# Attention scores from two 12-bit float32 parts in 64-row halves, in place of three bfloat16 parts in 32-column strips

## The chip, the cores and the metric

The kernel runs on one core of a Trainium2 chip, in one launch. The metric is the device time of that core in microseconds (us). Three runs of the kernel before gave 1925.89 us in the median, 1922.76 us at the lowest and 1926.48 us at the highest. TensorE multiplies matrices (PE in the profile; PEld is its loading of the stationary operand), VectorE (DVE), ScalarE (ACT) and GpSimd (POOL) work on rows of 128 partitions, and SyncE (SP) issues DMAs.

## The reference

Four layers of attention and a feed-forward part over 2048 tokens of width 128 follow one another; each adds attention times a gate to its input. The change lies in the two layers with 16 heads of width 8, layer 0 (all keys) and layer 3 (causal, with rotary positions). All is float32.

```python
def _L0_attn_ref(x, Wq, bq, Wk, bk, Wv, bv, Wo, bo):        # 16 heads, d = 8, T = 2048
    q, k, v = proj(Wq, bq), proj(Wk, bk), proj(Wv, bv)
    scores = jnp.einsum('bhtd,bhsd->bhts', q, k) * scale
    attn = jax.nn.softmax(scores, axis=-1)
    out = jnp.einsum('bhts,bhsd->bhtd', attn, v)
def _L3_attn_ref(x, qw, kw, vw, ow):
    Q, K = rope(Q, freq), rope(K, freq)
    score = jnp.einsum('bhqd,bhkd->bhqk', Q, K) / scale
    score = score - 10000000000.0 * (1.0 - causal)
    score = score - jnp.max(score, axis=-1, keepdims=True)
    weights = jax.nn.softmax(score, axis=-1)
    attn = jnp.einsum('bhqk,bhkd->bhqd', weights, V)
```

## The kernel before

`head_projections` makes q and k for all heads (128 rows, 8 per head) in eight blocks of 512 columns and splits each float32 number into three bfloat16 parts: ScalarE rounds the number (L403) and the rest (L407), VectorE subtracts (L446, L452). Six DMAs (L336) write the parts to memory outside the chip's buffers. `attention_heads` then runs the 16 heads. For one head, `load_stacks` puts the parts one above the other on 72 partitions, so that one product over 72 rows is the exact sum of the nine products of parts; `qs` holds the queries, `ks` the keys. In layer 0 a second pair, `qd` and `kd`, has the first 64 rows again on partitions 64 to 127.

Each head is gone through twice. The first pass finds the maximum of every query's scores. `fill` multiplies 128 queries by a block of 512 keys into `pM`: in layer 0 over 64 rows, two blocks side by side in the two halves of TensorE's rows (L747), in layer 3 over 72 rows, as four matmuls of 32 columns each (`by_columns`, L725). VectorE's `take` reduces the result (L881 over two blocks in layer 0, L892 and L889 over one in layer 3). `pM` has four banks in layer 0 and three in layer 3, and `fill` waits for the `take` that frees its bank. The 16 x 128 maxima of a head are split in three (`split_max`), turned by TensorE (`turn`, L757), copied by ScalarE (`keep_rows`, L837) and put by three DMAs (L639) on rows 72 to 74 of `qs`, where `ks` has ones: the second pass has the maximum subtracted by the product itself.

The second pass, `score_chunk`, multiplies 128 keys by 512 queries over 75 rows into `pS` (L725, four matmuls of 32 columns), ScalarE's exponential (L856) writes `probs`, and `sum_unit` multiplies four of those chunks by the values in float32, each chunk in a 32-column strip of its own (L787). A float32 product is two MATMUL records per strip. Four chunks are a unit; a head has 16 units in layer 0 and 10 in layer 3. `pS` has three banks: a score waits for the exponential three before it. In the causal layer a product with `neg_below` is added to a chunk that crosses the diagonal.

The order of TensorE's instructions is written out in `one_head` of the tensor block: the sums of unit u, then four scores (one of unit u+1 and three of unit u+2), with fills of the next head put between them at the places in `behind`. In layer 0 a unit has two fills: both behind the second score in even units, behind the first and the third in odd ones. In layer 3 a unit has three to five, and where there are four or more the last stands behind the fourth score, right before the next sums.

## Time and profile before

| | us |
|---|---|
| median of three runs | 1925.89 |
| lowest to highest | 1922.76 to 1926.48 |
| span of the profiled execution | 1923.2 |
| TensorE, VectorE, ScalarE busy in it | 1697.7, 1435.9, 1143.8 |

The profiled execution's time is its span of 1923.2 us from the first to the last instruction; the page gives nothing outside it, and the median of the runs is 2.7 us more. The heads of layer 0 run from about 55 to 740 us, those of layer 3 from about 1401 to 1840 us. TensorE's busy time counts a matmul from its start to its modelled end, so matmuls that follow one another overlap: the distance between two starts tells what a matmul costs in a stream, its duration does not. In the rows, an engine's name with a q (SPq) is its queue of DMA issues, and the bracket at a row's end is the idle time before it and what ended that.

### The profile page before, as it was taken

What the parts mean: (1) busy time and instruction counts of PE and PEld (TensorE: products, weight loads), DVE (VectorE), ACT (ScalarE), POOL (GpSimd) and SP (SyncE); (2) the same over time, 40 slices, a digit from 0 to 9 for tenths busy, and PEclk for the clock granted to TensorE, in tenths of its full rate; (3) what the DMA queues carried; (4) which work ended last, traced back from release to release, by engine and by line L of the source; (5) the groups of instructions that cost most, each with busy time, mean ns of one, the idle gap of its engine ahead of it and who ended that gap; (6) DMA issues with size and microseconds to landing.
All of it is one profiled execution on the core that took longest, in us unless ns stands there. A gap on an engine that the chain in (4) does not pass through costs nothing. (4 is left out here: it accounts for less than half of the span.)

```text
span 1923.2 us, 44062 instructions
## 1 busy us (share of the span) xinstructions
PE 1697.7 (88%) x17529; PEld 802.7 (42%) x17529; DVE 1435.9 (75%) x2718; ACT 1143.8 (59%) x2262; POOL 307.7 (16%) x460
## 2 busy tenths in 40 slices
PE   3799999999999995889997798892779999999977
PEld 2222222222222222434444544781425555555556
DVE  5889999999999954665555507656779999999735
ACT  3268888888888894332222244452317777777754
POOL 0103000010000100000000345443012232210123
PEclk8789999999999998799997899996759999999988
DMA  4112111121111012033233269861511111111132
GB/s 143 36 30 81 63 55 51 55 81 64 55 51 34 28 28 59 33 66 106 95 89 144 69 225 333 268 186 48 191 33 30 33 37 37 34 36 36 28 76 70
DMA packets 78037, 154.52 MB, mean 80 GB/s; under 512 B 18684, under 2 KB 35964, under 8 KB 74136
## 3 DMA queue, kind: packets, MB, share of 16 engines
q1 hardware_dynamic: 63034, 121.38, 20.0%
q0 software_dynamic: 14384, 29.29, 4.9%
q8 instruction: 139, 2.28, 0.5%
q10 hardware_dynamic: 414, 1.04, 0.2%
q14 instruction: 66, 0.54, 0.1%
HBM read 102.23 MB, written 48.89 MB: 79 GB/s over the span
## 5 line engine op out<-in xcount | busy, mean ns | idle before, releaser
L856 ACT ACTIVATE heads_probs<-heads_pS 128x512 f32<-128x512 f32 (+3 forms) x1664 | 851.6, 573 | 187.9 <-PE heads_pS L725 172.2
L881 DVE TENSOR_REDUCE heads_run_max<-heads_pM 128x1 f32<-128x1024 f32 x512 | 592.6, 1216 | 54.6 <-PE heads_pM L747 53.3
L787 PE MATMUL heads_pO<-heads_probs,heads_vh 128*32 128x512 f32 (+2 forms) x3328 | 438.1, 570 | 3.2 <-ACT heads_probs L856 1.4
L725 PE MATMUL heads_pS<-heads_qs,heads_ks 75*32 75x512 bf16 (+3 forms) x4160 | 392.7, 370 | 3.8 <-ACT heads_probs L856 1.6
L892 DVE TENSOR_REDUCE heads_run_max<-heads_pM 128x1 f32<-128x512 f32 x384 | 246.7, 684 | 17.2 <-PE heads_pM L725 13.7
L725 PE MATMUL heads_pS<-heads_q_first,heads_ks 75*32 75x512 bf16 x2496 | 234.4, 377 | 7.9 <-ACT heads_probs L856 7.4
L725 PEld LDWEIGHTS heads_pS<-heads_qs,heads_ks 75*32 75x32 bf16 x4160 | 117.3, 95 | 171.2 <-issue 81.3
L725 PE MATMUL heads_pM<-heads_ks,heads_qs 72*32 72x512 bf16 (+3 forms) x1600 | 174.6, 359 | 1.1 <-DVE heads_run_max L892 0.5
L889 DVE CUSTOM_DVE_ANT_0 heads_masked_out<-heads_pM,heads_mask_end 128x128 bf16<-128x128 f32 (+3 forms) x256 | 120.7, 485 | 19.5 <-PE heads_pM L725 17.2
L787 PEld LDWEIGHTS heads_pO<-heads_probs,heads_vh 128*32 128x32 f32 x3328 | 106.7, 110 | 53.3 <-issue 7.1
L725 PEld LDWEIGHTS heads_pS<-heads_q_first,heads_ks 75*32 75x32 bf16 x2496 | 71.3, 95 | 122.4 <-ACT heads_probs L856 66.8
L1404 ACT ACTIVATE top_act_gate<-top_pG 128x512 f32<-128x512 f32 x68 | 40.6, 597 | 137.3 <-PE top_pU L1360 137.3
L617 POOL DMA_DIRECT2D k_head_out_dram<-heads_ot x120 | 62.9, 531 | 356.9 <-DVE heads_ot L912 230.4
L747 PE MATMUL heads_pM<-heads_ks,heads_qs 64*128 64x512 bf16 x320 | 114.3, 393 | 4.7 <-DVE heads_run_max L881 4.7
L747 PE MATMUL heads_pM<-heads_kd,heads_qd 64*128 64x512 bf16 x320 | 114.3, 393 | 0.0
L725 PE MATMUL heads_pM<-heads_ks,heads_q_first 72*32 72x512 bf16 (+3 forms) x960 | 106.7, 383 | 7.9 <-DMA heads_ks<-k_parts_dram 6.7
L1438 DVE TENSOR_TENSOR top_hidden<-top_act_gate,top_pU 128x512 f32<-128x512 f32 x68 | 46.7, 687 | 76.8 <-ACT top_act_gate L1404 76.8
L2115 POOL DMA_INDIRECT k_x_slots_dram<-k_xn,k_place_i x32 | 31.1, 973 | 381.6 <-DVE k_place_i L1984 358.3
L725 PE MATMUL heads_pS<-k_neg_below,k_ident_b 128*32 128x128 bf16 x1024 | 90.7, 222 | 0.0
L1616 DVE TENSOR_REDUCE second_row_max<-second_banks 128x1 f32<-128x2048 f32 (+15 forms) x16 | 20.7, 1291 | 90.4 <-PE second_banks L1574 90.4
L725 PEld LDWEIGHTS heads_pM<-heads_ks,heads_qs 72*32 72x32 bf16 x1600 | 62.5, 97 | 59.3 <-DVE heads_run_max L892 19.1
L747 PEld LDWEIGHTS heads_pM<-heads_ks,heads_qs 64*128 64x128 bf16 x320 | 29.6, 93 | 133.4 <-DVE heads_run_max L881 86.7
(388 smaller groups left out, 2369.0 us busy)
## 6 DMA issues: line engine op xcount, KB each, us to landing
top_weights<-k_comb_dram SPq DMA_DIRECT2D x128, 128.0 KB, 3.0
second_w<-in_L_W_dram SPq DMA_DIRECT2D x12, 1024.0 KB, 10.8
k_hid_slots_dram<-k_zeros SPq DMA_DIRECT2D x8, 1152.0 KB, 5.0
k_h_slots_dram<-second_work SPq DMA_DIRECT2D x48, 192.0 KB, 3.1
second_work<-k_hid_slots_dram SPq DMA_DIRECT2D x48, 192.0 KB, 4.3
k_parts_dram<-proj_part SPq DMA_DIRECT2D x12, 512.0 KB, 4.1
heads_ks<-k_parts_dram SPq DMA_DIRECT2D x63, 96.0 KB
heads_qs<-k_parts_dram SPq DMA_DIRECT2D x40, 96.0 KB
```

The costliest lines, as they stand in the source:

```text
L617: queue.dma_start(K.head_out[h, :, b * BLK:(b + 1) * BLK], ot[c][b * 32:b * 32 + HD + 1, 0, :])\
L725: mm = pe.matmul(out[cols, :], still[:, cols], moving, start=start, stop=stop)
L747: mm = pe.matmul(pM[:, bank_of(c, j, k), 0:w], (qs, qd)[k][c % ROUND][rows, i * P:(i + 1) * P], (ks, kd)[k][c % ROUND][rows, b * BLK:b * B ...
L787: mm = pe.matmul(pO[k * 32:k * 32 + VW, int(second), o:BLK], vh[c][:, t, :], probs[u % 2][:, k * BLK + o:(k + 1) * BLK], start=first_chunk ...
L856: act.activation(probs[u % 2][:, k * BLK + c0 - b * BLK:(k + 1) * BLK], pS[:, slot, 0:c1 - c0], ACT.Exp)\
L881: dve.reduce_max(run_max[:, i, blocks[0][0] // 2:blocks[0][0] // 2 + 1], both.rearrange("p k c -> p (k c)"), AX.X).then_inc(taken, 2)
L889: dve.tensor_tensor_reduce(masked_out[:, i % TPB, 0:w], pM[:, bank, 0:w], mask_end[:, BLK - w:BLK], 1.0, LOWEST, ALU.add, ALU.max, run_max ...
L892: dve.reduce_max(run_max[:, i, b:b + 1], pM[:, bank, 0:w], AX.X).then_inc(taken, 1)
L1404: act.activation(act_gate[:, m % 2, :], pG[:, m % 2, :], ACT.Silu).then_inc(gated, 1)
L1438: mix = dve.tensor_tensor(hidden[:, m % 2, :], act_gate[:, m % 2, :], pU[:, m % 2, :], ALU.mult)
L1616: chain(dve.reduce_max(self.row_max[:, i:i + 1], self.scores_row[:, 0:(i + 1) * P], AX.X))
L2115: pool.indirect_dma_start(out=K.x_slots[k], out_offset=bass.IndirectOffsetOnAxis(ap=K.place_i[:, c, t:t + 1], axis=0), in_=K.xn[:, t, :], ...
```

## The change

Each number is split in two parts of 12 significant bits, held as float32 and declared as `float32r` (`ROUNDED`). VectorE masks the low bits (`HIGH_BITS`) and subtracts; ScalarE copies the masked part. Four products of parts make 32 rows (`STK`). Every head's stack lies twice, on partitions 0 to 63 and 64 to 127, and `fill` and `score_chunk` use the two halves in turn (`turns`). Row 32 is zero in the queries and one in the keys; the three rows of maxima are 33 to 35, written in both halves by six DMAs. `fill` multiplies over 33 rows, `score_chunk` over 36, each as one matmul of 128 columns; `by_columns`, `qd` and `kd` go. The causal mask is two bfloat16 products over one half's 64 rows, the second with the other half's mask (`ident_swapped`, `neg_below_swapped`). A head's stacks are 6 DMAs where there were 14 in layer 0 and 8 in layer 3. The spare rows are set by four memsets per buffer, on VectorE for the first buffer and GpSimd for two others, in place of one each. In layer 0 both fills of a unit stand behind its second score in every unit.

```diff
+ROUNDED = mybir.dt.float32r
...
 PARTS = 3
-STK = PARTS * PARTS * HD
+SPLIT = 2
+HIGH_BITS = -4096
+STK = SPLIT * SPLIT * HD
+HALF = 64
+MAX_ROW = STK + 1
...
-        parts = [[S.sb(f"part{w}{a}", [P, T], BF16) for a in range(PARTS)] for w in range(2)]
+        parts = [[S.sb(f"part{w}{a}", [P, T], ROUNDED) for a in range(SPLIT)] for w in range(2)]
...
+                for a, done in enumerate((hi, lo)):
                     sp.wait_ge(done, NB * (w + 1))
-                    sp.dma_start(K.parts[w][:, a, :, :], parts[w][a][:, :]).then_inc(stored[w], 16)
+                    sp.dma_start(K.parts[w][:, a, :, :], parts[w][a][:, :].bitcast(F32)).then_inc(stored[w], 16)
...
-                if n < N:
-                    act.wait_ge(whole, n + 1)
-                    act.activation(parts[w][0][:, cols], full[:, n % 4, :], ACT.Copy).then_inc(hi, 1)
                 if n >= 1:
                     w, b = divmod(n - 1, NB)
-                    act.wait_ge(r1, n)
-                    act.activation(parts[w][1][:, b * BLK:(b + 1) * BLK], rest[:, (n - 1) % 4, :], ACT.Copy)\
-                       .then_inc(mid, 1)
+                    act.wait_ge(masked, n)
+                    act.activation(parts[w][0][:, b * BLK:(b + 1) * BLK], rest[:, (n - 1) % 4, :], ACT.Copy)\
+                       .then_inc(hi, 1)
...
-                    w, b = divmod(n, NB)
-                    dve.wait_ge(hi, n + 1)
+                    dve.wait_ge(whole, n + 1)
                     if n >= 4:
-                        dve.wait_ge(lo, n - 3)
-                    dve.tensor_tensor(rest[:, n % 4, :], full[:, n % 4, :], parts[w][0][:, b * BLK:(b + 1) * BLK],
-                                      ALU.subtract).then_inc(r1, 1)
+                        dve.wait_ge(hi, n - 3)
+                    dve.tensor_scalar(rest[:, n % 4, :].bitcast(I32), full[:, n % 4, :].bitcast(I32), HIGH_BITS, None,
+                                      ALU.bitwise_and).then_inc(masked, 1)
                 if n >= 1:
                     w, b = divmod(n - 1, NB)
-                    cols = slice(b * BLK, (b + 1) * BLK)
-                    dve.wait_ge(mid, n)
-                    dve.tensor_tensor(parts[w][2][:, cols], rest[:, (n - 1) % 4, :], parts[w][1][:, cols],
-                                      ALU.subtract).then_inc(lo, 1)
+                    dve.wait_ge(masked, n)
+                    dve.tensor_tensor(parts[w][1][:, b * BLK:(b + 1) * BLK], full[:, (n - 1) % 4, :],
+                                      rest[:, (n - 1) % 4, :], ALU.subtract).then_inc(lo, 1)
...
 def first_queries(K, causal):
 
-    at = 0
-    for _, n0, n1 in PRODUCTS:
-        rows = at + (n1 - n0) * HD
-        for first in (0,) if causal or at >= HALF else (0, HALF):
-            yield K.first_q[first // HALF][first + at:first + rows, :], K.parts[0][0, n0:n1].rearrange("a d t -> d a t")
-        at = rows
+    for half in (0, HALF):
+        yield K.first_q[half:half + STK, :].bitcast(F32), query_parts(K, 0)
...
-        qs = [K.first_q[0]] + [S.sb(f"qs{i}", [P, T], BF16) for i in range(1, ROUND)]
-        ks = [S.sb(f"ks{i}", [P, T], BF16) for i in range(ROUND)]
-
-        qd = None if causal else [K.first_q[1]] + [S.sb(f"qd{i}", [P, T], BF16) for i in range(1, ROUND)]
-        kd = None if causal else [S.sb(f"kd{i}", [P, T], BF16) for i in range(ROUND)]
+        qs = [K.first_q] + [S.sb(f"qs{i}", [P, T], ROUNDED) for i in range(1, ROUND)]
+        ks = [S.sb(f"ks{i}", [P, T], ROUNDED) for i in range(ROUND)]
...
-        LOADS = 8 if causal else 14
+        LOADS, SPARE_ROWS = 6, 4
...
-            h, at = ROUND * p + c, 0
-            for r, n0, n1 in PRODUCTS:
-                n = n1 - n0
-                q = K.parts[0][h, n0:n1].rearrange("a d t -> d a t")
-                k = K.parts[1][h, r].unsqueeze(1).broadcast_to([HD, n, T])
-                for first in (0,) if causal or at >= HALF else (0, HALF):
-                    rows = slice(first + at, first + at + n * HD)
-                    for full, half, src in ((qs, qd, q), (ks, kd, k)):
-                        yield (half if first else full)[c % ROUND][rows, :], src, stacked[c % ROUND]
-                at += n * HD
+            h = ROUND * p + c
+            for half in (0, HALF):
+                yield qs[c % ROUND][half:half + STK, :].bitcast(F32), query_parts(K, h), stacked[c % ROUND]
+                for r in range(SPLIT):
+                    rows = slice(half + r * SPLIT * HD, half + (r + 1) * SPLIT * HD)
+                    yield ks[c % ROUND][rows, :].bitcast(F32), key_part(K, h, r), stacked[c % ROUND]
...
+        def set_spare_rows(engine, i):
+
+            for n, (stack, half) in enumerate(itertools.product((qs[i], ks[i]), (0, HALF))):
+                rows = slice(half + HALF // 2, half + HALF)
+                engine.memset(stack[rows, :].bitcast(F32), float(n // 2)).then_inc(rows_set[i], 1)
+                engine.wait_ge(rows_set[i], n + 1)
...
-                for a in range(PARTS):
-                    sp.dma_start(qs[c % ROUND][STK + a:STK + a + 1, :].rearrange("o (t c) -> o t c", c=P),
-                                 max_rows[a * NT:(a + 1) * NT, :]).then_inc(rows_in, 16)
+                for row in (MAX_ROW, HALF + MAX_ROW):
+                    for a in range(PARTS):
+                        sp.dma_start(qs[c % ROUND][row + a:row + a + 1, :].bitcast(F32).rearrange("o (t c) -> o t c", c=P),
+                                     max_rows[a * NT:(a + 1) * NT, :].bitcast(F32)).then_inc(rows_in, 16)
...
                     for i, (dst, src, sem) in enumerate(load_stacks(p, c + 2)):
-                        sp.wait_ge(scored, EVENTS * (ROUND * p + c) + 2 + 2 * i)
+                        sp.wait_ge(scored, EVENTS * (ROUND * p + c) + 2 + 4 * i)
                         sp.dma_start(dst, src).then_inc(sem, 16)
...
         @block.tensor
         def _(pe):
-            def by_columns(out, still, moving, start, stop):
-
-                for g in range(P // VW):
-                    cols = slice(g * VW, (g + 1) * VW)
-                    mm = pe.matmul(out[cols, :], still[:, cols], moving, start=start, stop=stop)
-                return mm
+            turns = itertools.cycle((0, HALF))
...
@@ -733,19 +728,15 @@
                 n = BLOCKS * (ROUND * p + c) + before[j + 1]
                 i, blocks, _ = runs[j]
                 if j == 0:
+                    pe.wait_ge(rows_set[c % ROUND], SPARE_ROWS)
                     pe.wait_ge(stacked[c % ROUND], 16 * LOADS * (p + c // ROUND + 1))
                 if not isinstance(n, int) or n > FILLED:
                     pe.wait_ge(taken, n - FILLED)
-                if causal:
-                    (b, w), = blocks
-                    bank = pM[:, bank_of(c, j, 0), :]
-                    mm = by_columns(bank[:, 0:w], qs[c % ROUND][0:STK, i * P:(i + 1) * P],
-                                    ks[c % ROUND][0:STK, b * BLK:b * BLK + w], True, True)
-                else:
-                    for k, (b, w) in enumerate(blocks):
-                        rows = slice(k * HALF, (k + 1) * HALF)
-                        mm = pe.matmul(pM[:, bank_of(c, j, k), 0:w], (qs, qd)[k][c % ROUND][rows, i * P:(i + 1) * P],
-                                       (ks, kd)[k][c % ROUND][rows, b * BLK:b * BLK + w], start=True, stop=True)
+                for k, (b, w) in enumerate(blocks):
+                    at = next(turns)
+                    rows = slice(at, at + STK + 1)
+                    mm = pe.matmul(pM[:, bank_of(c, j, k), 0:w], qs[c % ROUND][rows, i * P:(i + 1) * P],
+                                   ks[c % ROUND][rows, b * BLK:b * BLK + w], start=True, stop=True)
                 mm.then_inc(filled, 1)
...
                 diag = causal and c0 == u * P
-                mm = by_columns(pS[:, slot, 0:c1 - c0], ks[c % ROUND][0:STK + PARTS, u * P:(u + 1) * P],
-                                qs[c % ROUND][0:STK + PARTS, c0:c1], True, not diag)
+                at = next(turns)
+                rows, mask = slice(at, at + MAX_ROW + PARTS), slice(at, at + HALF)
+                mm = pe.matmul(pS[:, slot, 0:c1 - c0], ks[c % ROUND][rows, u * P:(u + 1) * P],
+                               qs[c % ROUND][rows, c0:c1], start=True, stop=not diag)
                 if diag:
-                    mm = by_columns(pS[:, slot, 0:P], K.ident_b[:, :], K.neg_below[:, :], False, True)
+                    pe.matmul(pS[:, slot, 0:P], K.ident_b[mask, :], K.neg_below[mask, :], start=False, stop=False)
+                    mm = pe.matmul(pS[:, slot, 0:P], K.ident_swapped[mask, :], K.neg_below_swapped[mask, :], start=False,
+                                   stop=True)
                 mm.then_inc(scored, 1)
...
                     else:
 
-                        behind = [(len(new) // 2, 1 + 2 * i)[u % 2] for i in range(len(todo))]
+                        behind = [len(new) // 2] * len(todo)
...
-            dve.memset(ks[0][64:96, :], 1.0).then_inc(ones_set[0], 1)
+            set_spare_rows(dve, 0)
```

The first place is TensorE's queue in layer 0, from one unit's sums to the next (an odd unit before). heads_pO are the sums, heads_pS the scores, heads_pM the maxima's products. Before:

```order
L787 MATMUL heads_pO<-heads_probs,heads_vh 32x512 x4
L725 MATMUL heads_pS<-heads_q_first,heads_ks 32x512 x4
L747 MATMUL heads_pM<-heads_ks,heads_qs 128x512
L747 MATMUL heads_pM<-heads_kd,heads_qd 128x512
L725 MATMUL heads_pS<-heads_q_first,heads_ks 32x512 x8
L747 MATMUL heads_pM<-heads_ks,heads_qs 128x512
L747 MATMUL heads_pM<-heads_kd,heads_qd 128x512
L725 MATMUL heads_pS<-heads_q_first,heads_ks 32x512 x4
L787 MATMUL heads_pO<-heads_probs,heads_vh 32x512 x4
```

The same stretch of the changed kernel:

```order
L782 MATMUL heads_pO<-heads_probs,heads_vh 32x512 x4
L764 MATMUL heads_pS<-heads_q_first,heads_ks 128x512 x2
L738 MATMUL heads_pM<-heads_ks,heads_qs 128x512 x4
L764 MATMUL heads_pS<-heads_q_first,heads_ks 128x512 x2
L782 MATMUL heads_pO<-heads_probs,heads_vh 32x512 x4
```

The four strips of a score are one matmul now, and the four products for the maxima stand together between the second and the third score; sums in 32-column strips stand between work of 128 columns on both sides.

The second place is TensorE's queue in layer 3, up to the sums of a unit with a fill right before them. Before:

```order
L725 MATMUL heads_pM<-heads_ks,heads_q_first 32x512 x4
L725 MATMUL heads_pS<-heads_qs,heads_ks 32x256 x4
L725 MATMUL heads_pS<-k_neg_below,k_ident_b 32x128 x4
L725 MATMUL heads_pM<-heads_ks,heads_q_first 32x512 x4
L725 MATMUL heads_pS<-heads_qs,heads_ks 32x512 x4
L725 MATMUL heads_pM<-heads_ks,heads_q_first 32x512 x4
L787 MATMUL heads_pO<-heads_probs,heads_vh 32x384 x2
```

The same place of the changed kernel:

```order
L738 MATMUL heads_pM<-heads_ks,heads_qs 128x512
L764 MATMUL heads_pS<-heads_qs,heads_ks 128x256
L767 MATMUL heads_pS<-k_neg_below,k_ident_b 128x128
L768 MATMUL heads_pS<-k_neg_below_swapped,k_ident_swapped 128x128
L738 MATMUL heads_pM<-heads_ks,heads_qs 128x512
L764 MATMUL heads_pS<-heads_qs,heads_ks 128x512
L738 MATMUL heads_pM<-heads_ks,heads_qs 128x512
L782 MATMUL heads_pO<-heads_probs,heads_vh 32x384 x2
```

The order of fills and scores is the same; all of them were in 32-column strips like the sums, and none is now.

## Rows read from the trace of the kernel before

**Rows 1.** Engine totals of 50 us in the heads of layer 0 and of layer 3:
```profile
200.00:250.00 50.00, 50.00 (x565) 14.41 (x561) 46.36 (x42) 43.90 (x83) 3.21 (x9) 1.00 0.16 52
...
1650.00:1700.00 50.00, 49.62 (x902) 28.23 (x898) 45.97 (x123) 36.73 (x80) 6.28 (x12) 1.00 0.12 27
```

**Rows 2.** Timeline of layer 0, two units; start us, us, engine line:
```profile
400.19 1.03 PE L787 MATMUL heads_pO<-heads_probs,heads_vh 128*32 128x512 f32 x8
...
401.59 0.39 PE L747 MATMUL heads_pM<-heads_ks,heads_qs 64*128 64x512 bf16 x1
...
401.82 0.38 PE L747 MATMUL heads_pM<-heads_ks,heads_qs 64*128 64x512 bf16 x1
...
404.62 0.09 PEld L747 LDWEIGHTS heads_pM<-heads_ks,heads_qs 64*128 64x128 bf16 x1 [0.42 <-DVE heads_run_max L881]
...
404.94 0.40 PE L725 MATMUL heads_pS<-heads_qs,heads_ks 75*32 75x512 bf16 x4
...
405.17 0.60 PE L787 MATMUL heads_pO<-heads_probs,heads_vh 128*32 128x512 f32 x4
```

**Rows 3.** Timeline of VectorE, maxima of layer 0 with every bank full:
```profile
71.06 22.71 DVE L881 TENSOR_REDUCE heads_run_max<-heads_pM 128x1 f32<-128x1024 f32 x20 [0.17 <-PE heads_pM L747]
```

**Rows 4.** Timeline of the last head of layer 0, TensorE:
```profile
705.78 0.40 PE L725 MATMUL heads_pS<-heads_qs,heads_ks 75*32 75x512 bf16 x4 [0.27 <-ACT heads_probs L856]
...
706.01 1.03 PE L787 MATMUL heads_pO<-heads_probs,heads_vh 128*32 128x512 f32 x8
...
706.87 0.39 PE L725 MATMUL heads_pS<-heads_qs,heads_ks 75*32 75x512 bf16 x4
...
707.96 0.40 PE L725 MATMUL heads_pS<-heads_q_first,heads_ks 75*32 75x512 bf16 x4 [0.27 <-ACT heads_probs L856]
```

**Rows 5.** Timeline of ScalarE, layer 3, once per head:
```profile
1585.30 0.27 ACT L837 ACTIVATE heads_max_rows<-heads_pS 48x128 bf16<-48x128 bf16 x1 [0.71 <-PE heads_pS L757]
...
1611.33 0.27 ACT L837 ACTIVATE heads_max_rows<-heads_pS 48x128 bf16<-48x128 bf16 x1 [0.71 <-PE heads_pS L757]
```

**Rows 6.** Timeline of TensorE, bf16 maxima and then f32 products:
```profile
63.05 0.38 PE L747 MATMUL heads_pM<-heads_ks,heads_q_first 64*128 64x512 bf16 x1
...
63.36 0.49 PE L963 MATMUL heads_pS<-k_squares,heads_probs 128*128 128x128 f32 x2
...
63.68 0.39 PE L964 MATMUL heads_pS<-k_rows_of,k_ident 128*128 128x128 f32 x2
...
63.91 0.39 PE L963 MATMUL heads_pS<-k_squares,heads_probs 128*128 128x128 f32 x2
```

**Rows 7.** Timeline of layer 1, f32 products behind a wait and in stream:
```profile
920.26 1.12 PE L1368 MATMUL top_pY<-top_hidden,k_down 128*128 128x512 f32 x2 [0.54 <-DVE top_hidden L1444]
...
921.22 1.02 PE L1359 MATMUL top_pG<-k_xnT,k_gate 128*128 128x512 f32 x2
...
922.08 1.02 PE L1360 MATMUL top_pU<-k_xnT,k_up 128*128 128x512 f32 x2
```

**Rows 8.** Timeline, layer 0, from the maxima's transpose to the next head:
```profile
300.98 1.84 SPq L639 DMA_DIRECT2D heads_qs<-heads_max_rows  x3
...
305.71 0.61 PE L725 MATMUL heads_pS<-heads_qs,heads_ks 75*32 75x512 bf16 x8
```

**Rows 9.** What the loads of the maxima (L639) took in layer 0:
```profile
DMA to landing us min/median/max: 1.7/1.7/3.3
```

**Rows 10.** Timeline, layer 3, start of the heads stage:
```profile
1400.29 0.11 DVE L923 MEMSET heads_run_max<- 128x64 f32 x1
...
1401.71 1.85 PE L725 MATMUL heads_pM<-heads_ks,heads_q_first 72*32 72x128 bf16 x24 [6.71 <-DMA heads_ks<-k_parts_dram]
```

**Rows 11.** Groups of instructions of the first 50 us:
```profile
L403 ACT ACTIVATE proj_part<-proj_full 128x512 bf16<-128x512 f32 x8 | 5.0, 630 | 0.3
...
L114 DVE MEMSET k_zeros<- 128x2304 f32 x1 | 2.0, 1978 | 1.3 <-PEq L2606 1.3
L917 DVE MEMSET heads_ks<- 32x2048 bf16 x1 | 1.8, 1765 | 3.5 <-PEq L65 3.5
```

57 lines of the change are left out of this document (28 added, 29 removed).

## The prediction

> **What bounds the kernel now.** I read the engine totals in stretches first, then the timeline of each of the two heads stages, then the nearest relatives of what the change adds. In the heads of layer 0 TensorE is busy in all 50.00 us of 50, VectorE in 46.36, ScalarE in 43.90; in layer 3 it is 49.62, 45.97 and 36.73 [rows 1]. TensorE's share alone says little, since its matmuls overlap, so the timeline decides. In layer 0 the sums of one unit start at 400.19 us and those of the second unit after it at 405.17: 2.49 us a unit [rows 2]. VectorE could go faster: with every bank full it does 20 reductions of 1024 in 22.71 us, 1.14 us each, 2.27 us a unit [rows 3]. What would be left without the maxima is seen in the last head, where nothing is filled: the score in front of the sums starts at 705.78, the next such score at 707.96, a cycle of 2.18 us [rows 4]. It is closed: that score waits for an exponential, the sums follow 0.23 us behind it, the next score 0.86 us behind the sums' start, and 1.09 us later the exponential of that score has released the next one. So a unit in layer 0 costs 2.49 us through TensorE's own stream, with 2.27 (VectorE) and 2.18 (the cycle) right below it. In layer 3 a head takes 1611.33 - 1585.30 = 26.03 us, 2.60 us for each of ten units [rows 5]. There a maximum's product of 512 columns stands between the last score and the sums in most units, so the cycle is 2.18 + 0.21 = 2.39 us (the granted clock is 1.00, the level of 2.4 GHz [rows 1], and 512 columns at that are 0.21 us); the other 0.21 are masks, narrow pieces and the turn of a head.
>
> **Part 1: the width of the products.** In a stream, two pairs of bf16 products of 64 rows and 512 columns start 0.23 us apart [rows 2], and the two of a pair run together. The new products are of a type that the trace doesn't show. The nearest rows below are these bf16 pairs (one pass over the columns), above them the f32 products, whose two records cost 922.08 - 921.22 = 0.86 us, four passes [rows 7]. A part has only 12 bits, and nothing in the change calls for a second half of it, so I take one pass, and I take it that two products in different halves overlap as the bf16 pairs do. Then eight products of a unit in layer 0 take four times 0.21 us where six slots did the same before (four scores, two pairs): TensorE's stream falls by 0.43 us a unit and is no bound any more. What comes next is the cycle through the sums.
>
> **Part 2: what the cycle gets longer by.** Before, scores and sums were both in 32-column strips in both layers; now sums stand between products of 64 rows and 128 columns. (a) From products of one shape to the other costs 0.10 us: a bf16 pair is started at 404.62, the strips behind it at 404.94, 0.32 us in place of the 0.23 between two pairs [rows 2]. (b) The way back is dearer, since the stationary operand is four bytes wide: bf16 products at 63.05, f32 at 63.36 (0.31, so 0.10 again), and the next at 63.68, 0.32 us behind in place of the 0.23 from there to 63.91 [rows 6]. 0.10 + 0.10 = 0.20 us. (c) The score in front of the sums waits for its exponential, and only then can its weights be loaded. For f32 that shows: 920.26 to 921.22 is 0.96 us behind a wait, 0.86 in the stream [rows 7], 0.10 us; for bf16 it doesn't (the load at 404.62 ends a wait for VectorE [rows 2], and the 0.32 from there to the next product is 0.01 more than the 0.31 of a pair that hadn't waited [rows 6]). I take 0.10. Together 0.10 + 0.20 + 0.10 = 0.40 us, and the cycle is 2.18 + 0.40 = 2.58 us. The bounds of (b) and (c): if the new type's weights load as bf16 does, the load costs 0 in both and the sum is 0.20; if in (a) the sums' weights also have to be loaded with nothing beside them, 0.10 more, 0.50.
>
> The Trainium skill (TensorEngine Tiling (Array Packing), Key Properties) says that a change of tiling mode, other than one of tile, drains TensorE. The trace agrees, with the 0.10 us of [rows 2, 6]; by that rule alone, the cycle would be 2.38 us.
>
> The Trainium skill (TensorE: Matmul & The Clock Gate, Weight-path perf modes) says that the fast load of weights is on for 128 weights of a type other than FP32. The trace agrees as far as it goes: 0.10 us for f32, none for bf16 [rows 6, 7]; no run here shows on which side `float32r` stands. On the fast side the sum would be the one of rival B.
>
> **Part 3: the sum.** Layer 0: 2.58 - 2.49 = 0.09 us a unit, 15 heads of 16 units, +22 us. The last head has no maxima and goes from 2.18 to 2.58: 16 x 0.40 = +6. The maxima before the first head's scores are VectorE's [rows 3] and stay. Layer 3: the maximum's product between score and sums now runs beside the score, in the other half, but its weights are loaded behind the score's, 0.10 us (c). So the cycle goes from 2.39 to 2.68, +0.29 us; ten units and 15 heads, +44, and the last head +4. I keep the 0.21 of masks and narrow pieces as it is: the mask's two products are 0.05 us each in one half instead of one such, hidden where the other half has work. The order of layer 0's maxima costs and brings nothing, as TensorE has slack there.
>
> **Part 4: the ends.** Six DMAs of maxima in place of three: three are issued in 1.84 us [rows 8], six in 3.7, and one lands 1.7 us after its issue [rows 9], so the last lands at 300.98 + 3.05 + 1.7 = 305.7; the next head's first score is the second of those from 305.71 on [rows 8]. Just in time, 0; if they come late by all three issues, 1.84 x 30 heads = +55 is the far bound, nothing the near one. Memsets: VectorE sets 2304 columns of f32 in 1.98 us and 2048 of bf16 in 1.77 [rows 11], the same rate, so three more are 5.3 us. In layer 3 VectorE was ready at 1400.40, the first product started at 1401.71 [rows 10]: 1400.40 + 5.3 - 1401.71 = +4. In layer 0 the feed-forward products stand in front, 0. GpSimd's memsets are needed only when the second head's maxima start, some 20 us later. The projections lose one cast of 0.63 us for each of eight blocks [rows 11] and store 4 MB in place of 3: -5 to +3 for both layers, I take -3. The head stacks are 1 MB as before, at a DMA share of 0.16 and 0.12 [rows 1]: 0.
>
> Sum: 22 + 6 + 44 + 4 + 4 - 3 = +77 us on a span of 1923.2, 2000 us; the median of the runs is 2.7 us above that span, so 2003, rounded to 2000.
>
> **Rivals.** B, the loads don't show, on the other side: the new type's weights load like bf16. Cycle 2.38 us. Layer 0 gains 0.11 x 240 = 26 and loses 3 in the last head; layer 3 goes from 2.39 to 2.38, gains 2, loses 2; with the ends -22: 1904. If the change of shape costs nothing either, VectorE is the bound: 2.27 in layer 0 (-0.22 x 240 = -53) and 45.97 / 50 of the time in layer 3 (26.03 x 15 x 0.08 = -31), about 1842. B decides as soon as the cycle grows by less than 2.49 - 2.18 = 0.31 in layer 0 and 0.21 in layer 3. For it: only f32 rows show the load. Against: the operand is four bytes wide as theirs is. C, the halves don't overlap for this type (that the change doesn't do what it is laid out for): a unit of layer 0 is eight products of 0.21, sums of 0.86 and two changes, 1.7 + 0.86 + 0.3 = 2.86 us, +0.37 x 240 = 89; in layer 3 the maximum's product is in line again as before, and the rest grows by the 0.30 of the changes, +0.30 x 150 = 45; with the last heads' 10, 144, 2070. For it: nothing in the trace shows two four-byte products in halves. Against: eight records of f32 products in strips take 1.03 us together [rows 4]. D, two passes or more: a score of two passes is 0.21 us longer, and the cycle has two of them, before the sums and behind: 2.58 + 0.42 = 3.00 in layer 0 (+0.51 x 240 = 122) and 2.68 + 0.42 = 3.10 in layer 3 (+0.71 x 150 = 107), the last heads 26 x 0.82 = 21, so 2180; with four passes 250 more. E, gains and losses meet within 4 us, between A and B.
>
> **Chances.** My forecast A 0.46 (its own range 1970 to 2035), B 0.27, C 0.13, D 0.08, E 0.06. The time is A's, 2000. The range for 8 in 10 goes from 1895, which has B but for its far end, to 2070, where C is. A measurement of this kernel tells 0.2% (4 us) from no change. Faster 0.28, same 0.06, slower 0.66.
>
> **What would show it.** Right: in layer 0 the sums' starts are 2.5 to 2.65 us apart in every unit alike; the last head's cycle is near 2.58; ScalarE waits for TensorE's scores in each unit; VectorE is busy below 46 of 50 us; a head of layer 3 takes 28 to 29 us. B: the last head's cycle is 2.4 or less and VectorE is above 48 of 50. C: two scores side by side start 0.2 us apart, not 0.01. D: the same score's matmuls in one half start 0.4 us or more apart, or have two records. The forecast is wrong if the last head's cycle is not longer by 0.3 to 0.5 us.

## The result: 2645 us, 37% slower, at half of TensorE's clock

The changed kernel takes 2645.22 us (median of 4 runs, 2643.52 to 2646.26), the kernel before, on the same chip, 1926.18 us (4 runs, 1922.76 to 1927.63). The ratio is 1.374, with a 95% interval of 1.372 to 1.376. The forecast was 2000 us with a range to 2070: the sign was right, the size missed by 645 us.

The page's slices of the changed kernel show where to look. Each digit is a slice of 66 us, busy tenths of TensorE above, its granted clock in tenths below:

```profile
PE   3799999999999999977999698943999999999987
...
PEclk8555555555555555557999799976555555555558
```

Through the heads of layer 0 (slices 2 to 18) and of layer 3 (29 to 39) the clock is 0.50, the level of 1.2 GHz. TensorE is not idle there: in slices 3 to 17 and 29 to 38 it is busy in nine tenths and more. In windows (columns as in [rows 1]: PE, PEld, DVE, ACT, POOL, clock, DMA share, GB/s):

```profile
500.00:550.00 50.00, 50.00 (x199) 20.01 (x201) 29.48 (x27) 27.77 (x52) 3.20 (x9) 0.50 0.13 48
...
1300.00:1450.00 150.00, 148.40 (x354) 65.54 (x353) 84.53 (x132) 35.06 (x60) 0.00 (x0) 1.00 0.28 85
...
2000.00:2050.00 50.00, 50.00 (x230) 20.35 (x226) 28.21 (x74) 23.90 (x49) 7.37 (x11) 0.50 0.10 29
```

The middle one is layer 1, whose code the change leaves alone: clock 1.00. The outer two answer to [rows 1], where it was 1.00 too. VectorE and ScalarE, 46 and 44 of 50 before, are at 29 and 28: they wait for TensorE, ScalarE for 766 us in all (the last entry of this group of the page):

```profile
L851 ACT ACTIVATE heads_probs<-heads_pS 128x512 f32<-128x512 f32 (+3 forms) x1664 | 875.0, 571 | 799.4 <-PE heads_pS L764 766.0
```

The timeline of TensorE answers to [rows 2]; the first sums start at 500.21, the next at 504.28, so a unit (four chunks of scores and their sums) takes 4.07 us in place of 2.49. The last three rows are from layer 3:

```profile
500.21 1.93 PE L782 MATMUL heads_pO<-heads_probs,heads_vh 128*32 128x512 f32 x8
502.08 0.79 PE L764 MATMUL heads_pS<-heads_qs,heads_ks 36*128 36x512 f32 x2
502.67 1.05 PE L738 MATMUL heads_pM<-heads_ks,heads_qs 33*128 33x512 f32 x4
503.53 0.82 PE L764 MATMUL heads_pS<-heads_qs,heads_ks 36*128 36x512 f32 x2
504.28 1.08 PE L782 MATMUL heads_pO<-heads_probs,heads_vh 128*32 128x512 f32 x4
...
2051.05 0.62 PE L764 MATMUL heads_pS<-heads_qs,heads_ks 36*128 36x512 f32 x1
2051.05 0.62 PE L738 MATMUL heads_pM<-heads_ks,heads_qs 33*128 33x512 f32 x1
2051.48 0.62 PE L764 MATMUL heads_pS<-heads_qs,heads_ks 36*128 36x512 f32 x1
```

Even the sums, which are the same instructions as before, take 1.93 us in place of 1.03. The last three rows answer part 1 of the prediction: two products in different halves start together, and the next score in its half starts 0.43 us later. 512 columns at 1.2 GHz are 0.43 us: one pass. So rivals C and D are out, and what all the heads have in common is the clock; experiments 1 and 13 measure how much of the excess it is. A head of layer 3 takes 1955.57 - 1912.24 = 43.33 us (26.03 in [rows 5]):

```profile
1912.24 0.27 ACT L832 ACTIVATE heads_max_rows<-heads_pS 48x128 fp32r<-48x128 bf16 x1 [1.51 <-PE heads_pS L748]
1955.57 0.27 ACT L832 ACTIVATE heads_max_rows<-heads_pS 48x128 fp32r<-48x128 bf16 x1 [1.51 <-PE heads_pS L748]
```

One more wait is new. TensorE's waits, in total, times, longest:

```profile
PE heads_pM L738 <- DMA heads_ks<-k_parts_dram: 44.8, 2, 29.6
```

At the start of each of the two stages the first maximum waits for the stacks of keys, 15.1 us in layer 0 and 29.6 us in layer 3. In the kernel before that wait is 6.71 us in layer 3 [rows 10].

### The profile page after: what moved, and what is told of

Read it like the earlier page. It is cut to its first block and busy times, and to the rows that moved or that the text cites. A ratio compares the mean times of both kernels' runs of the same rounds, so it can differ in the third digit from the quotient of the medians.

```text
span 2642.9 us, 29151 instructions
## 1 busy us (share of the span) xinstructions
PE 2393.8 (91%) x10105; PEld 1100.5 (42%) x10105; DVE 1461.2 (55%) x2728; ACT 1159.3 (44%) x2246; POOL 328.2 (12%) x472
## 5 line engine op out<-in xcount | busy, mean ns | idle before, releaser
L782 PE MATMUL heads_pO<-heads_probs,heads_vh 128*32 128x512 f32 (+2 forms) x3328 | 804.6, 1012 | 1.4 <-ACT heads_probs L851 1.4
L764 PE MATMUL heads_pS<-heads_qs,heads_ks 36*128 36x512 f32 (+3 forms) x1040 | 497.6, 716 | 1.3 <-ACT heads_probs L851 1.3
L764 PEld LDWEIGHTS heads_pS<-heads_qs,heads_ks 36*128 36x128 f32 x1040 | 258.3, 302 | 451.4 <-ACT heads_probs L851 254.8
L738 PE MATMUL heads_pM<-heads_ks,heads_qs 33*128 33x512 f32 (+3 forms) x1040 | 390.0, 642 | 3.8 <-DVE heads_run_max L876 3.3
L764 PE MATMUL heads_pS<-heads_q_first,heads_ks 36*128 36x512 f32 x624 | 303.6, 717 | 6.6 <-ACT heads_probs L851 6.4
L738 PE MATMUL heads_pM<-heads_ks,heads_q_first 33*128 33x512 f32 x624 | 235.4, 647 | 53.3 <-DMA heads_ks<-k_parts_dram 44.8
L764 PEld LDWEIGHTS heads_pS<-heads_q_first,heads_ks 36*128 36x128 f32 x624 | 151.6, 301 | 287.8 <-ACT heads_probs L851 148.2
L738 PEld LDWEIGHTS heads_pM<-heads_ks,heads_qs 33*128 33x128 f32 x1040 | 214.7, 318 | 41.6 <-DVE heads_run_max L887 8.8
L738 PEld LDWEIGHTS heads_pM<-heads_ks,heads_q_first 33*128 33x128 f32 x624 | 126.9, 311 | 90.9 <-issue 49.2
L767 PE MATMUL heads_pS<-k_neg_below,k_ident_b 64*128 64x128 bf16 x256 | 83.7, 327 | 0.0
```

Of the source, the lines that this page charges most:

```text
L738: mm = pe.matmul(pM[:, bank_of(c, j, k), 0:w], qs[c % ROUND][rows, i * P:(i + 1) * P], ks[c % ROUND][rows, b * BLK:b * BLK + w], start=Tru ...
L764: mm = pe.matmul(pS[:, slot, 0:c1 - c0], ks[c % ROUND][rows, u * P:(u + 1) * P], qs[c % ROUND][rows, c0:c1], start=True, stop=not diag)
L767: pe.matmul(pS[:, slot, 0:P], K.ident_b[mask, :], K.neg_below[mask, :], start=False, stop=False)
L782: mm = pe.matmul(pO[k * 32:k * 32 + VW, int(second), o:BLK], vh[c][:, t, :], probs[u % 2][:, k * BLK + o:(k + 1) * BLK], start=first_chunk ...
```

## The experiments

They ran on four other chips than the first comparison: experiments 1 to 4 on one, 5 to 8, 9 to 12 and 13 to 15 on one each. The kernel before takes 1997.1, 1997.8, 1993.9 and 1999.5 us there, so every comparison below is with a run on one of these chips, and one across two of them can be off by up to 6 us. Experiments 9, 10, 11 and 15 have four to six runs each, the others one. "Unit" is the time from one unit's sums to the next in layer 0.

**1. All 64 rows of a half.** There are three theories of why the clock stays low. R: because a product has few rows (33 or 36) at work. T: because of the four-byte type. S: because the low level keeps itself, once the engine has waited.

```diff
-                    rows = slice(at, at + STK + 1)
+                    rows = slice(at, at + HALF)
...
-                rows, mask = slice(at, at + MAX_ROW + PARTS), slice(at, at + HALF)
+                rows, mask = slice(at, at + HALF), slice(at, at + HALF)
```

> Every product of a maximum and every score reads all 64 rows of its half (33 and 36 before); the spare rows hold zeros against ones, and in a maximum's product the rows of the head three back, which only shifts all scores of a row. Same records, same widths. Theory R (few rows of the array are at work, and so the granted clock stays at 0.50 in the heads): with 64 rows the clock is 1.00 again in 500-550 us of layer 0, a unit takes 2.4 to 2.7 us in place of 4.07, the kernel 1850 to 2070 us. Theory T (the four-byte type holds it down) and theory S (the slow level keeps itself, since the engine waits between its products): clock 0.50, unit 4.07 us, time 2640 within 15 us.

Measured: 2176.6 us, clock 1.00 in layer 0, unit 504.56 - 501.97 = 2.59 us. The spare rows hold zeros against ones, so they add nothing to a score (in a maximum's product, rows 33 to 35 hold the maxima of the head three back, which shift all scores of a query alike); that they are read is enough. The window of 50 us, and then the timeline of TensorE in this kernel:

```profile
500.00:550.00 50.00, 49.78 (x310) 18.27 (x306) 44.73 (x40) 40.43 (x80) 3.19 (x9) 1.00 0.18 70
```

```profile
501.97 1.06 PE L782 MATMUL heads_pO<-heads_probs,heads_vh 128*32 128x512 f32 x8
502.96 0.50 PE L764 MATMUL heads_pS<-heads_qs,heads_ks 64*128 64x512 f32 x2
503.30 0.82 PE L738 MATMUL heads_pM<-heads_ks,heads_qs 64*128 64x512 f32 x4
503.96 0.67 PE L764 MATMUL heads_pS<-heads_qs,heads_ks 64*128 64x512 f32 x2
504.56 1.07 PE L782 MATMUL heads_pO<-heads_probs,heads_vh 128*32 128x512 f32 x8
...
1691.22 0.44 PE L738 MATMUL heads_pM<-heads_ks,heads_qs 64*128 64x128 f32 x1 [5.11 <-issue]
```

So theory R holds, and the 2.59 is the 2.58 of my part 2. The total is above my 1850 to 2070, for layer 3 is still slow: its clock is 0.86 to 0.93, and once a head TensorE waits up to 5.4 us (62.9 us in 14 heads) in front of a maximum of the next stack but one, as in the last row. That is taken up in experiment 5.

**2. The type alone, and 3. type and rows.** Both operands are read as bf16 with a stride of two (`stack.bitcast(BF16)`, every second element), with 33 and 36 rows, and with 64. These two kernels leave the lower bits of every part out of the computation; only their times are of use.

> The same products with the same 33 and 36 rows in the same halves and the same order, but both operands are read as the upper two bytes of each element, bf16 with a stride of two (the lower bits are left out of the computation). Theory T (the type): clock 1.00, unit near 2.4 to 2.7 us, kernel 1850 to 2070 us. Theories R (rows) and S (keeps itself): clock 0.50; a unit of about 4 us, 2550 to 2650 us, and what it is shorter than 4.07 is what the loads of the wider type cost at the lower level.

> Both edits at once: bf16 operands read with a stride of two, and all 64 rows of the half. In the kernel before, pairs of such products stood among strips at a clock of 1.00 [rows 1, 2]. Theories R and T each say clock 1.00 here and 1850 to 2070 us; only theory S (the level keeps itself once the engine waits, whatever its operands are) says clock 0.50 and about 2600 us.

Measured: 2344.2 us with the few rows, 2114.2 us with 64. With the few rows the clock is 0.50 up to 530 us, and then, without any edit there, 1.00 up to the last head. Windows of that kernel:

```profile
300.00:350.00 50.00, 50.00 (x219) 9.63 (x213) 32.24 (x29) 29.70 (x56) 3.20 (x9) 0.50 0.06 23
...
600.00:650.00 50.00, 46.72 (x328) 10.02 (x326) 48.01 (x44) 43.41 (x85) 4.02 (x13) 1.00 0.13 48
```

My expectation for few rows (2550 to 2650) missed for this reason: with bf16 either level can hold for hundreds of us. So T is not refuted as a contribution, though the type alone doesn't bring the clock back for good. The total with 64 rows is above my 1850 to 2070, with the same waits in layer 3 as in experiment 1 (82.4 us in 14 heads). With 64 rows the clock is 1.00 throughout the heads of layer 0, and the unit is 2.41 to 2.42 us, the 2.38 of rival B. The loads of weights can explain the 0.17 between the two types (groups by shape, mean ns behind the busy time; first the kernel with 64 rows of the four-byte type, then bf16, then f32 products of layer 1 in the kernel before):

```profile
L764 PEld LDWEIGHTS heads_pS<-heads_q_first,heads_ks 64*128 64x128 f32 x64 | 9.1, 184 | 16.6 <-ACT heads_probs L851 16.3
```

```profile
L767 PEld LDWEIGHTS heads_pS<-heads_q_first,heads_ks 64*128 64x128 bf16 x31 | 2.3, 94 | 7.7 <-ACT heads_probs L854 7.5
```

```profile
L1368 PEld LDWEIGHTS top_pY<-top_hidden,k_down 128*128 128x128 f32 x72 | 13.4, 188 | 19.1 <-DVE top_hidden L1444 13.2 <-issue 3.3
```

That is 0.09 us for each load, and by part 2 two of them stand in a cycle with nothing beside them. Experiment 11 tests it: with stacks that really are bf16 the unit is 2.39 us.

**4. No halves, 128 rows.** Both copies are summed at once, which gives twice the score, and the exponential halves it: `rows = slice(0, P)`, `scale=0.5`. A maximum's product has 97 rows.

> No halves: each product reads rows 0 to 127 of the stacks (0 to 96 for a maximum), so both copies are summed at once, twice the score, and the exponential halves it. Products of 128 rows can't run beside each other. Theory R: 99 and 128 rows at work, clock 1.00; a unit of layer 0 is eight products of 0.21, sums 0.86, changes 0.3, so about 2.9 us, the kernel 2050 to 2150 us. Theories T and S: clock 0.50, a unit of 8 x 0.43 + 1.9 = 5.3 us or more, the kernel about 3000 us. If a product takes 0.86 us at a clock of 0.50, a product of 128 rows of this type needs two passes.

Measured: 2295.0 us, clock 1.00 in both layers, unit 503.89 - 500.83 = 3.06 us. Again theory R. The total is above my 2050 to 2150: I had left out the waits for the stacks (45.5 us at the two starts) and the slower chip, and the unit is 3.06 in place of my 2.9. It also shows what the halves are worth: 3.06 against 2.59 us.

**5. The loads of the stacks.** In the changed kernel a DMA of a stack has an outermost dimension of 2 (the copies). In a window of the changed kernel where nothing else is loaded (DMA share and GB/s are the last two numbers) the share of the 16 DMA engines is 0.13, which is 2 of 16:

```profile
60.00:66.00 6.00, 0.00 (x0) 0.00 (x0) 0.00 (x0) 0.00 (x0) 3.44 (x8) 0.50 0.13 52
```

The edit gives it the 8 rows of a part, as in the kernel before. A head then has eight loads of 16 rows in place of six, and its rows stand in another order:

```diff
-    return K.parts[0][h].rearrange("a d t -> (a d) t").unsqueeze(0).broadcast_to([SPLIT, SPLIT * HD, T])
+    return K.parts[0][h].rearrange("a d t -> d a t")
...
-    return K.parts[1][h, r].unsqueeze(0).broadcast_to([SPLIT, HD, T])
+    return K.parts[1][h, r].unsqueeze(1).broadcast_to([HD, SPLIT, T])
```

> The kernel with 64 rows in every product, and its stacks loaded in eight DMAs a head of 16 rows whose outermost dimension is the 8 rows of a part (six DMAs whose outermost dimension is 2 before; the rows of a stack stand in another order, the sums are the same). Theory L (a DMA is spread over as many engines as its outermost dimension allows, 2 of 16 before, so a head's 1 MB takes near 20 us and comes late): the wait of 16 us before the first maximum of each of the two layers falls below 5 us, the waits of 4 to 5 us in each head of layer 3 (62.9 us in 14) go, the kernel is 80 to 100 us shorter than 2176.6, so 2075 to 2095. Theory Q (the issues on SyncE, 1.57 us each for the keys, are what is late): the waits stay within a quarter of what they are, 2150 to 2190 us.

Measured: 2066.5 us, 110 less. TensorE no longer waits for stacks, layer 3's clock is 1.00, and a head of it takes 27.85 us where nothing disturbs it (1899.07 - 1871.12 = 27.95 below). Windows of this kernel (the first: the loads, at half of the DMA engines), then TensorE in the last head of layer 0, then ScalarE once per head of layer 3:

```profile
50.00:60.00 10.00, 8.43 (x19) 3.05 (x17) 7.80 (x8) 4.18 (x7) 9.71 (x6) 0.82 0.51 118
...
1800.00:1850.00 50.00, 47.06 (x352) 20.33 (x352) 42.69 (x114) 33.49 (x75) 5.96 (x11) 1.00 0.18 46
```

```profile
741.94 1.07 PE L782 MATMUL heads_pO<-heads_probs,heads_vh 128*32 128x512 f32 x8
...
744.55 0.64 PE L782 MATMUL heads_pO<-heads_probs,heads_vh 128*32 128x512 f32 x4
```

```profile
1871.12 0.27 ACT L832 ACTIVATE heads_max_rows<-heads_pS 48x128 fp32r<-48x128 bf16 x1 [0.64 <-PE heads_pS L748]
1899.07 0.27 ACT L832 ACTIVATE heads_max_rows<-heads_pS 48x128 fp32r<-48x128 bf16 x1 [0.64 <-PE heads_pS L748]
```

The total is below my 2075 to 2095. The edit changed the issues on SyncE too: the two of keys behind one another took 3.15 us in the kernel of experiment 1 (the row below), one takes 0.65 now. So it doesn't part L from Q by itself, but the row does: that load had been issued by 1678.48 + 3.15 = 1681.63 us, and the maximum that waited for it started at 1691.22, 9.6 us later. The transfer was late, not the issue.

```profile
1678.48 3.15 SPq L649 DMA_DIRECT2D heads_ks<-k_parts_dram  x2
```

At the start of layer 3 TensorE still sits idle for 19.6 us before its first maximum, now until VectorE's memsets are done (part 4 below). The Trainium skill (DMA: Bandwidth & Descriptors, Why a DMA increments its semaphore by 16 and not by 1) says that a DMA uses the largest number of engines up to 16 that divides the slowest dimension of both of its access patterns. The shares of 0.13 with 2 and 0.51 with 8 agree, and I had not applied it.

**6. A push at the start.** 40 products of 128 rows of f32 ahead of each layer's first head.

> The changed kernel, and in each of the two layers 40 products of 128 rows and 128 columns of f32 once, ahead of the first head's scores (their output is overwritten). Theory S (the level keeps itself, it only has to be brought up once): the clock is 1.00 behind them and stays so through the layer's heads, near 2.6 us a unit, 2100 to 2200 us. Theory R (rows): the clock goes to 1.00 during the 40 products at most and is back at 0.50 a few units later; the kernel takes 2640 to 2670 us.

Measured: 2723.5 us, above my 2640 to 2670; the changed kernel itself takes 2707.0 on another of these chips (14). Windows around the push:

```profile
132.00:136.00 4.00, 4.00 (x38) 3.88 (x37) 0.00 (x0) 0.00 (x0) 0.00 (x0) 1.00 0.00 0
136.00:140.00 4.00, 3.55 (x17) 1.11 (x17) 0.00 (x0) 3.54 (x7) 0.00 (x0) 0.99 0.06 16
140.00:144.00 4.00, 4.00 (x18) 1.58 (x18) 2.36 (x2) 2.17 (x4) 0.00 (x0) 0.50 0.14 57
```

The push ends at 135.9 us. TensorE waits once more, 0.45 us before the score at 137.03, and from there on not at all; up to 140 the clock is 0.99, behind it 0.50, with TensorE busy in all of the window. So raising the level once isn't enough: for the four-byte products of few rows theory S is out as a full account, since they let the clock fall from above.

**7. and 8. Only one of the two kinds with 64 rows.** One of the two lines of the first edit each.

> Only the products of the maxima read 64 rows, the scores stay at 36. Theory R with the sum of all rows deciding: four of eight products of a unit of layer 0 are full, the clock is at one level or the other for long stretches, mean between 0.6 and 0.9, 2250 to 2500 us. If either kind alone is enough, 2180 us; if both are needed, 2640.

> Only the scores read 64 rows, the products of the maxima stay at 33. In layer 0 this is the same number of wide products as with the maxima at 64 rows, so by the sum of all rows the same clock and time as there; in the last head of each layer, where only scores stand, the clock is 1.00.

Measured: 2232.0 and 2226.4 us. In layer 0 either alone is enough: clock 1.00 in 500:550 and a unit near 2.60 us in both. In layer 3 (1800:1850) it is 0.77 in both, below the 0.93 of experiment 1; but both kernels also wait for their stacks there (49.0 and 41.9 us), so these runs don't show what one kind alone would do in layer 3 without those waits. The last head of layer 0, where only scores stand, tells the two apart; the maxima with 64 rows, then the scores with 64 rows:

```profile
750.00:800.00 50.00, 46.23 (x160) 12.08 (x161) 1.75 (x1) 27.79 (x54) 2.08 (x4) 0.55 0.20 47
```

```profile
750.00:800.00 50.00, 42.65 (x242) 13.19 (x240) 9.04 (x8) 40.30 (x79) 2.91 (x8) 1.00 0.20 48
```

As soon as only 36-row scores are left, the clock falls; with 64-row scores it doesn't.

**9. Both mendings, and 10. both with the old order of the maxima.** The first is the kernel of experiment 5 once more. The second sets `behind` back to `[(len(new) // 2, 1 + 2 * i)[u % 2] for i in range(len(todo))]`.

> The kernel with 64 rows in every product and loads of eight outer rows once more, timed. By the single look (2064.6 us of span, the kernel before 1997.8 on the same chip) the ratio is 1.03; by the prediction's own sum (+77 us on 1923) it would be 1.04. If both mendings are all that the forecast had missed, the ratio lies between 1.025 and 1.045.

> The same kernel with layer 0's maxima in the order of the kernel before (every second unit takes its two runs of maxima behind the first and the third score). Theory N (the order is worth nothing, as I forecast, since the cycle through the sums decides): within 0.2% of the kernel with the new order. Theory O (the maxima's weight loads hide between scores that wait for their exponentials): a pair between two scores that wait anyway costs nothing, while the pair of sums' neighbours moves: up to 0.1 us in every second unit, 12 us faster. Theory P (a pair ahead of the score that the sums wait for makes the cycle longer in every second unit): 0.2 us in 120 units, 24 us slower.

Measured: 2069.5 and 2074.4 us, 1.0374 (1.0357 to 1.0391) and 1.0397 (1.0379 to 1.0414) of the kernel before. The 15 heads of layer 0, from the first keeping of maxima to the last, take 640.3 us in the new order and 639.7 in the old: in the place that it changes, the order is worth nothing. The 5 us between the totals, just over my 0.2%, lie elsewhere: of the 8.4 us between the two profiled spans, 4.7 are between the attention layers and 3.3 in layer 3, where both kernels have the same instructions. They were not looked into.

**11. Six products of bf16 parts.** A version that might beat both: parts and loads as in the kernel before, but six of the nine products of parts (the three smallest are left out of the sum), 48 rows, alternating halves, all 64 rows read.

```diff
+STACK = ((0, 0, 3), (1, 3, 2), (2, 5, 1))
+STK = 6 * HD
...
+                for r, at, n in STACK:
+                    rows = slice(half + at * HD, half + (at + n) * HD)
+                    yield qs[c % ROUND][rows, :], query_parts(K, h, n), stacked[c % ROUND]
+                    yield ks[c % ROUND][rows, :], key_part(K, h, r, n), stacked[c % ROUND]
```

> A version that might beat both: three bf16 parts as in the kernel before, but only six of the nine products of parts (48 rows, with the spare and the maxima's rows 64), in both halves of the array in turn and with all 64 rows at work; twelve loads a head with 8 outer rows. If the 0.17 us a unit between the four-byte stacks (2.59) and the bf16 reading of them (2.42) is the load of the wider weights, a unit of layer 0 takes 2.41 us against 2.49 in the kernel before, -19 us in 240 units, the last head +4; in layer 3 a head goes from 27.85 to about 26.0, which is what the kernel before takes. Ratio to the kernel before 0.985 to 1.0. If what costs 0.17 us is something else about the four-byte stacks' traffic, the unit stays at 2.59 and the ratio is 1.03.

Measured: 1988.9 us, ratio 0.9972 (0.996 to 0.9985), 0.3% less than the kernel before, with a unit of 2.39 us. So stacks that are bf16 give about what the bf16 reading of four-byte stacks gave (2.41), as it should be if the load of the wider weights is what costs the 0.2 us. In 14 heads the first score waits for its maxima's rows, 13.1 us in all, the place that my part 4 called just in time.

**12. The kernel before, here.**

> The kernel before itself, with a profile on the chip of these runs, where it takes 1997 us and not 1926 as in the first comparison. Theory G (the 70 us belong to the chip and lie in the stages between the two attention layers, where the runs with 64 rows also took about 50 us more than the changed kernel did in the first comparison): the units of layer 0 are 2.49 us apart as before and a head of layer 3 takes 26.0 us. Theory H (the heads are slower on this chip too): a unit is longer by more than 0.05 us, and then the units of the other kernels have to be read against it.

Measured: 1994.7 us. The 15 heads of layer 0 take 607.0 us (607.1 in the first comparison), those of layer 3 413.1 (396.2), and from the last keeping of maxima in layer 0 to the first in layer 3 it is 773.6 us (722.0). So 52 of the 70 us lie between the two attention layers, and theory G holds for layer 0 and not wholly for layer 3, where the first eight heads take 28 to 31 us each on this chip and the last seven 26.0 to 26.4. What these chips do more slowly there was not looked into.

**13. The loads mended, 33 and 36 rows kept, and 14. the changed kernel itself, here.**

> The changed kernel with its 33 and 36 rows, and only the loads of the stacks mended (eight a head, 8 outer rows). Theory R + L (rows set the clock, loads come late only where the heads are fast or just starting): clock 0.50 in the heads as before, the waits before the first maximum of each layer go (44.8 us in 2 to under 15), none in between, so 25 to 40 us shorter than the changed kernel on this chip, which I put at 2715. Theory I (the clock fell because the engine waited for loads): clock 1.00 in the heads and about 2070 us.

> The changed kernel itself on the chip of these runs. The kernel before is 68 us longer here than in the first comparison, in the stages between the two attention layers. If that is the chip and not the kernel, the changed kernel takes 2700 to 2725 us here, with the units of layer 0 4.07 us apart and the clock 0.50 in the heads as there. If the clock of the heads is a matter of the chip, it is not 0.50 here.

Measured: 2681.0 and 2707.0 us on one chip, clock 0.50 in the heads of both. The loads are worth 26 us at the lower level (at the two starts the first maximum waits 46.8 us for loads, and with the loads mended 20.1 for VectorE's memsets), and 110 at the upper one (experiments 1 and 5), where a head is short enough to run into them. A mending in the loads alone doesn't bring the clock back.

**15. The six products again, with fewer issues.** One DMA for three rows of maxima, and blocks placed so that no load waits for a memset: `qs[...][row:row + PARTS, :].rearrange("a (t c) -> a t c", c=P)` from `max_rows[:, :]`, `STACK = ((0, 0, 3), (2, 3, 1), (1, 6, 2))`.

> The six products of parts once more, with two edits: the rows of the smallest block stand at 24 and those of the middle one at 48, so that the spare rows 32 to 47 can be set without a wait of the loads for it; and the three rows of maxima go in one DMA for each half, 2 in place of 6 a head. If the issues on SyncE are what is late, the wait for the maxima's rows (13.1 us in 14 heads of layer 0) and about half of the 13.8 us at the start of layer 3 go: 15 to 25 us less than 1988.9, ratio to the kernel before 0.985 to 0.992. If one DMA of three rows is slower than three of one, by more than the 2.5 us saved in issues, the ratio stays at 0.997.

Measured: 1968.8 us (5 runs), ratio 0.9839 (0.9825 to 0.9854), 1.6% less than the kernel before. The wait for the maxima's rows is gone. Which of the two edits gave how much of the 20 us isn't separated. The window of layer 0, TensorE's timeline of one unit there, and that of the last head, which has no maxima:

```profile
500.00:550.00 50.00, 47.20 (x337) 9.88 (x329) 49.00 (x44) 43.66 (x86) 3.19 (x9) 1.00 0.15 50
```

```profile
501.86 1.07 PE L788 MATMUL heads_pO<-heads_probs,heads_vh 128*32 128x512 f32 x8
...
504.25 1.07 PE L788 MATMUL heads_pO<-heads_probs,heads_vh 128*32 128x512 f32 x8
```

```profile
690.21 1.06 PE L788 MATMUL heads_pO<-heads_probs,heads_vh 128*32 128x512 f32 x8
...
692.60 1.06 PE L788 MATMUL heads_pO<-heads_probs,heads_vh 128*32 128x512 f32 x8
```

The 15 heads of layer 0 take 584.4 us against 607.0. VectorE is busy in 49.00 of 50, but it isn't the bound: in the last head, where it has next to nothing to do (1.75 us of the 30 from 685 to 715), the sums are 2.39 us apart as well. The bound is still the cycle through the sums, with VectorE right below it.

## Why the prediction was wrong, step by step

**The step that failed** is in part 1, and the prediction never wrote it as a step. It read "the granted clock is 1.00, the level of 2.4 GHz [rows 1]" in the kernel before, where the heads' products have 64, 72 and 75 rows, and priced the new products of 33 and 36 rows at that level (0.21 us for 512 columns, and all that parts 1 to 3 build on it). They run at 1.2 GHz: in the last head of layer 0 the cycle, forecast at 2.58 us, is 4.07 us (the sums start at 1153.08 and 1157.15), while the page shows a clock of 0.50. On the chips of the experiments, in spans, the changed kernel is 2705.2 - 1992.9 = 712 us above the one before. Of these the loads are 2705.2 - 2679.1 = 26, the rows 2679.1 - 2069.2 = 610, and 2069.2 - 1992.9 = 76 are left. (The 610 are taken across two chips that differ by 6 us in the kernel before; the 26 and the 76 are from one chip each.)

That the 76 meet the forecast sum of +77 is in good part luck, since its terms missed in both directions. Experiments 12 and 9 are on one chip:

| | forecast, us | measured, us |
|---|---|---|
| layer 0, 15 heads | +22 | 640.3 - 607.0 = +33 |
| last head of layer 0 | +6 | +7 |
| layer 3, 15 heads | +44 | 431.1 - 413.1 = +18 |
| last head of layer 3 and what follows | +4 | 108.9 - 104.6 = +4 |
| start, projections, memsets | +4 - 3 = +1 | 76 - 33 - 7 - 18 - 4 = +14 |

**Part 1** held but for the level: one pass, halves beside each other.

**Part 2** held at the upper level. Cycle in the last head 2.58 forecast, 744.55 - 741.94 = 2.61 measured; unit 2.58 and 2.59. The two loads of (b) and (c) were put at 0.10 each and measure 0.09. The question left open there, on which side of the Trainium skill's rule (TensorE: Matmul & The Clock Gate, Weight-path perf modes) `float32r` stands, is answered by 184 ns against 94: it loads like f32 (188 ns), without the fast load. The bf16 reading is 2.41 to 2.42 and the bf16 stacks 2.39, against 2.38 for rival B. So B's condition was not met, but its price was right.

**Part 3**: in layer 0 a unit is 2.60 us in place of 2.58, which against 2.49 is +26 over 240 units. The other 7 are 0.4 to 0.5 us more a head, at its turn (5.4 us of it are the waits for the maxima's rows, part 4). In layer 3 the undisturbed heads take 27.85 us against 26.03, which is +27 over 15 and not +44. The measured +18 is less still, since both kernels are held up in their first eight or nine heads there, the kernel before by 22 us and this one by 13. So the cycle of layer 3 was put 0.1 us too high. I had added a whole load for the maximum beside the score; that this is what is too much is my reading, and no run isolates it. The last head is 0.43 longer in each of 16 units, 7 us. The order of layer 0's maxima is worth nothing, as forecast.

**Part 4** failed in three terms. "The head stacks are 1 MB as before: 0" compared bytes and a mean DMA share, and not how many DMA engines a transfer is spread over; it cost 26 us in the changed kernel and would have cost 110 had the clock stayed.

"Just in time, 0" for the maxima's rows holds only at the lower level, where TensorE never waits for them. With the clock at 1.00 they are late: TensorE's waits in experiment 9 (total, times, longest) come to 10.5 us in 13 heads, against 3.1 us in 4 in experiment 12, and to 0.9 us a time in experiment 11:

```profile
PE heads_pS L764 <- DMA heads_qs<-heads_max_rows: 8.0, 9, 3.2
PE heads_pS L764 <- DMA heads_q_first<-heads_max_rows: 2.5, 4, 1.3
```

The ends were put at +1 and measure +14. In layer 3 the memsets cost what the forecast said: from VectorE's first memset to the first product it is 1452.33 - 1447.47 = 4.9 us in experiment 12 and 1505.42 - 1496.24 = 9.2 in experiment 9, +4.3. But the projections, put at -3, got longer: from the last subtraction's end to that first memset it is 6.0 us in experiment 12 and 13.3 in experiment 9, where the last store of parts is twice as large and is issued behind four loads, 4.8 us after that end. Layer 0, put at 0, reaches its first keeping of maxima at 98.3 us in place of 94.6. First experiment 12, then experiment 9:

```profile
1447.47 1.76 DVE L917 MEMSET heads_ks<- 32x2048 bf16 x1 [4.98 <-PEq L65]
...
1452.33 1.85 PE L725 MATMUL heads_pM<-heads_ks,heads_q_first 72*32 72x128 bf16 x24 [7.19 <-DMA heads_ks<-k_parts_dram]
```

```profile
1496.24 1.76 DVE L601 MEMSET heads_q_first<- 32x2048 f32 x1 [12.27 <-PEq L71]
...
1505.42 2.16 PE L738 MATMUL heads_pM<-heads_ks,heads_q_first 64*128 64x128 f32 x6 [19.17 <-DVE heads_run_max L918]
```

**What could have been seen ahead.** Nothing in the trace of the kernel before shows that rows count: it has no products of few rows. It does show that the clock of its heads can be at either level. In one stretch it is 0.50 while pairs of 64 rows wait for VectorE, and in the next it comes back with the full mix of scores, maxima and sums. Windows of the kernel before:

```profile
84.00:90.00 6.00, 3.30 (x12) 0.52 (x10) 6.00 (x6) 0.00 (x0) 0.00 (x0) 0.50 0.00 0
...
108.00:114.00 6.00, 6.00 (x60) 1.39 (x56) 3.51 (x4) 3.71 (x8) 0.00 (x0) 0.77 0.19 60
114.00:120.00 6.00, 6.00 (x72) 1.65 (x64) 5.54 (x6) 5.03 (x10) 0.00 (x0) 1.00 0.26 68
```

I had taken the clock for a matter of waiting alone, so I had no rival for it. Its condition could not be read from this trace, but its price could, from [rows 2, 4]: scores and sums at twice their time, 1.7 + 1.7 and the changes, near 4 us a unit, 2600 us and more.
